# Two stages of a Flamingo block: the last store of keys and values crosses the stage border, one weight split moves two tiles forward, one signal moves ahead of four loads

## The reference, cut to what matters

```python
x = x + tanh(g_xattn[0]) * L0_xattn(_layernorm(x), ctx, ...)     # stages 1, 2, 3
x = x + tanh(g_ffn[0])   * L0_ffn(_layernorm(x), ...)            # stages 4, 5
x = x + tanh(g_xattn[1]) * L1_xattn(_layernorm(x), ctx, ctx)     # stage 6
x = x + tanh(g_ffn[1])   * L1_ffn(_layernorm(x), ...)            # stage 7

# L0_xattn, 16 query heads over 4 key and value heads, head size 128:
q = rope(rms_norm(x @ wq)); k = rope(rms_norm(x @ wk)); v = x @ wv
k_ctx = rms_norm(ctx @ wk_ctx); v_ctx = ctx @ wv_ctx
p = softmax(q @ [k_ctx, k].T / sqrt(128) + causal)
out = (p @ [v_ctx, v]) @ wo
```

## Time and profile before

| | |
|---|---|
| median of three runs | 2157.63 us |
| the three runs | 2154.73, 2157.63, 2162.49 us |
| the profiled execution | 2155.77 us |
| its span in the profile | 2154.0 us |
| TensorE busy | 1963.9 us, 91% of the span |
| mean granted clock of TensorE | 0.967 of full speed |

### The profile page before, as it was taken

How to read it: one execution, slowest core, us unless ns; L and a number is a source line. 1 busy time by engine, 2 the same in 40 slices (tenths; PEclk the granted TensorE clock), 3 DMA queues, 4 the chain that set the end, 5 groups by cost and what they waited for, 6 DMA issues and landing times. The chain is left out here.

```text
span 2154.0 us, 33149 instructions
## 1 busy us (share of the span) xinstructions
PE 1963.9 (91%) x10498; PEld 1491.0 (69%) x10514; DVE 1344.3 (62%) x2408; ACT 1072.4 (50%) x2590; POOL 428.9 (20%) x515
## 2 busy tenths in 40 slices
PE   6999789999999999978998999999979978886898
PEld 5788667777777777756887778778768865554444
DVE  6777566666666666654342755555645437884886
ACT  3333356666656666653222312222324328984998
POOL 1111144444444444430000000000000001222111
PEclk9999899999999999999999999999989988997999
DMA  6776843333323240118443121112477422331121
GB/s 252 260 256 221 293 129 108 79 89 79 96 74 108 60 107 22 30 30 293 136 142 112 59 79 39 59 39 88 127 255 258 157 85 89 108 108 46 35 59 44
DMA packets 209016, 253.55 MB, mean 118 GB/s; under 512 B 12246, under 2 KB 158822, under 8 KB 202476
## 3 DMA queue, kind: packets, MB, share of 16 engines
q1 hardware_dynamic: 208876, 251.82, 36.7%
HBM read 151.10 MB, written 100.68 MB: 117 GB/s over the span
## 5 line engine op out<-in xcount | busy, mean ns | idle before, releaser
L966 ACT ACTIVATE at_prob<-at_S,at_bias,at_rq 128x384 f32<-128x384 f32 (+1 forms) x256 | 184.1, 731 | 142.9 <-DVE at_bias L1051 138.1
L1062 DVE TENSOR_TENSOR at_pt_lo<-at_PT,at_pt_hi 128x512 fp32r<-128x512 f32 x224 | 148.8, 688 | 92.3 <-ACT at_pt_hi L973 92.2
L835 POOL TENSOR_SCALAR at_prob<-at_prob,at_rsum 128x384 f32<-128x384 f32 (+1 forms) x256 | 160.3, 639 | 135.0 <-DVE at_rsum L1057 135.0
L1713 ACT ACTIVATE gu_silu<-gu_G 128x512 f32<-128x512 f32 x64 | 38.1, 596 | 245.3 <-PE gu_G L103 236.0
L1042 DVE TENSOR_REDUCE at_nmax<-at_S 128x1 f32<-128x384 f32 (+1 forms) x256 | 150.9, 617 | 9.5 <-PE at_S L885 5.5
L973 ACT ACTIVATE at_pt_hi<-at_PT 128x512 fp32r<-128x512 f32 x224 | 127.9, 604 | 53.8 <-PE at_PT L892 53.8
L892 PE MATMUL at_PT<-c_ident,at_prob 128*128 128x128 f32 x896 | 127.8, 277 | 21.1 <-DVE at_pt_lo L1062 20.8
L1750 DVE TENSOR_TENSOR gu_h<-gu_silu,gu_U 128x512 f32<-128x512 f32 x64 | 43.8, 686 | 151.6 <-PE gu_U L103 105.2
L824 POOL TENSOR_TENSOR at_q<-at_by_cos,at_by_sin 128x512 f32<-128x512 f32 x64 | 82.1, 1283 | 265.0 <-DVE at_by_sin L1034 152.5
L892 PEld LDWEIGHTS at_PT<-c_ident,at_prob 128*128 128x128 f32 x896 | 97.8, 140 | 50.9 <-DVE at_pt_lo L1062 46.5
L881 PE MATMUL at_S<-at_k_hi,at_q_hi 128*128 128x384 f32 (+1 forms) x256 | 113.2, 442 | 15.5 <-DVE at_q_lo L1067 11.5
(11 more groups left out here) (341 smaller groups left out, 5474.7 us busy)
## 6 DMA issues: line engine op xcount, KB each, us to landing
wide<-at_ot SPq DMA_DIRECT2D x64, 256.0 KB, 2.9
wide<-gu_h SPq DMA_DIRECT2D x64, 256.0 KB, 3.2
o_a<-wide SPq DMA_DIRECT2D x14, 1024.0 KB, 4.8
d_a<-wide SPq DMA_DIRECT2D x13, 1024.0 KB, 8.6
keys_hi<-kv_kt_hi SPq DMA_DIRECT2D x16, 512.0 KB, 3.3
keys_lo<-kv_kt_lo SPq DMA_DIRECT2D x16, 512.0 KB, 4.1
values_hi<-kv_v_hi SPq DMA_DIRECT2D x16, 512.0 KB, 4.7
values_lo<-kv_v_lo SPq DMA_DIRECT2D x16, 512.0 KB, 5.0
```

What stands on the lines that cost most here:

```text
L835: pool.tensor_scalar(prob[u % 2][:, h, 0:n], prob[u % 2][:, h, 0:n], rsum[:, s:s + 1], 1.0, ALU.mult, ALU.mult).then_inc(normed.sem, 1)
L966: act.activation(prob[u % 2][:, h, 0:n], S[h][:, 0:n], ACT.Exp, bias=bias[:, s:s + 1], scale=rq[u % 4][:, h:h + 1], accum_out=sums[:, s:s ...
L1062: dve.tensor_tensor(pt_lo[f % 4][:], bank_of("p", u, kb)[:], pt_hi[f % 4][:].bitcast(F32), ALU.subtract).then_inc(pt_done.sem, 1)
```

## The change

Four things change; the arithmetic and all values stay as they are.

- **Stores.** The last four stores of stage 1 (turn 3, n = 8) signal a semaphore of their own, `c.kv_last`, which stage 1 doesn't wait for. The buffers that they read (`kt_hi`, `kt_lo`, `v_hi`, `v_lo` of source 0) move to the right side and live through stage 2. There they serve as `prob`, `pt_hi` and `pt_lo`. SP waits for `kv_last` in stage 2, ahead of the loads of `wq` into `prob`.
- **Split.** The high and low parts of the first `wq` piece are taken after tile 5 of the last turn, not after tile 7.
- **Signal.** `xt_arrived` is signalled ahead of the four small loads.
- **keep_awake** at the end of stage 1 has 12 matmuls, not 24.

```diff
@@ keys_values
-        kt_hi = [mem.sb(f"kt_hi{s}", [P, HKV, TOK]) for s in range(SRC)]
-        kt_lo = [mem.sb(f"kt_lo{s}", [P, HKV, TOK]) for s in range(SRC)]
+        kt_hi = [c.kt_hi, mem.sb("kt_hi1", [P, HKV, TOK])]
+        kt_lo = [c.kt_lo, mem.sb("kt_lo1", [P, HKV, TOK])]
...
+        v_hi = [c.v_hi, mem.sb("v_hi1", [P, TT, HKV * HD], F32R)]
+        v_lo = [c.v_lo, mem.sb("v_lo1", [P, TT, HKV * HD], F32R)]
...
+                    stored = kv_stored[s].sem if more or n < NT else c.kv_last
                     wait_apart(sp, kt_done, turn, n, passed)
                     for dram, keys in ((scr.k_hi, kt_hi), (scr.k_lo, kt_lo)):
-                        sp.dma_start(dram[turn, s, :, :, tok], keys[s][:, :, tok]).then_inc(kv_stored[s].sem, 16)
+                        sp.dma_start(dram[turn, s, :, :, tok], keys[s][:, :, tok]).then_inc(stored, 16)
...
-            for s in (xt_stored, ct_stored, *kv_stored):
+            for s in (xt_stored, ct_stored, kv_stored[1]):
                 sp.wait_ge(s.sem, s.per * (PAIRS + 1))
+            sp.wait_ge(*kv_stored[0].at(PAIRS - 1, 64))
...
-            keep_awake(pe, T[0], c, 2 * AWAKE)
+            keep_awake(pe, T[0], c, AWAKE)
...
+            def split_queries_hi(i):
+                act.wait_ge(wq_arrived[i], 16)
+                act.wait_ge(*V_full.at(PAIRS - 1, TT))
+                act.activation(c.wq_hi[i][:], (x, cx)[i][:], ACT.Copy).then_inc(wq_hi_done, 1)
...
+                    if not more and i == TT + 1:
+                        split_queries_hi(0)
...
-            for i in range(2):
-                act.wait_ge(wq_arrived[i], 16)
-                act.wait_ge(*V_full.at(PAIRS - 1, TT))
-                act.activation(c.wq_hi[i][:], (x, cx)[i][:], ACT.Copy).then_inc(wq_hi_done, 1)
+            split_queries_hi(1)
...
+            def split_queries_lo(i):
+                dve.wait_ge(wq_hi_done, i + 1)
+                dve.tensor_tensor(c.wq_lo[i][:], (x, cx)[i][:], c.wq_hi[i][:].bitcast(F32),
+                                  ALU.subtract).then_inc(wq_lo_done, 1)
...
+                    if not more and i == TT + 1:
+                        split_queries_lo(0)
...
+            split_queries_lo(1)
@@ attention
+        mem.sems.append(c.kv_last)
...
-        prob = [mem.sb(f"prob{i}", [P, GROUP, 2 * L]) for i in range(2)]
+        prob = [c.kt_hi, c.kt_lo]
...
-        pt_hi = [mem.sb(f"pt_hi{i}", [P, GROUP * P], F32R) for i in range(4)]
-        pt_lo = [mem.sb(f"pt_lo{i}", [P, GROUP * P], F32R) for i in range(4)]
+        pt_hi = [c.v_hi[:, i, :] for i in range(4)]
+        pt_lo = [c.v_lo[:, i, :] for i in range(4)]
...
+            for b in range(2):
+                sp.sem_inc(xt_arrived[b].sem, 32)
             sp.dma_start(cosw[:], io["c_cos_tok"]).then_inc(setup, 16)
...
-            for b in range(2):
-                sp.sem_inc(xt_arrived[b].sem, 32)
             load_kv(0, 0, 0)
+
+            sp.wait_ge(c.kv_last, 4 * 16)
             for n in range(HKV - AHEAD):
                 weights.load(sp, n)
@@ make_queries
+        self.kt_hi, self.kt_lo = (far(f"kt_{part}", [P, HKV, TOK], F32) for part in ("hi", "lo"))
+        self.v_hi, self.v_lo = (far(f"v_{part}", [P, TT, HKV * HD]) for part in ("hi", "lo"))
+        self.kv_last = nc.alloc_semaphore("queries_kv_last")
```

More of the change, by code:

```diff
@@ L289, in keys_values @@
         kn = [mem.sb(f"kn{i}", [P, 512]) for i in range(2)]
-        v_hi = [mem.sb(f"v_hi{s}", [P, TT, HKV * HD], F32R) for s in range(SRC)]
-        v_lo = [mem.sb(f"v_lo{s}", [P, TT, HKV * HD], F32R) for s in range(SRC)]
+        v_hi = [c.v_hi, mem.sb("v_hi1", [P, TT, HKV * HD], F32R)]
+        v_lo = [c.v_lo, mem.sb("v_lo1", [P, TT, HKV * HD], F32R)]
         cosw = mem.sb("cosw", [P, 2, HD])
@@ L396, in body @@
                         sp.dma_start(dram[turn, s, :, tiles, :],
-                                     values[s][:, tiles, :].bitcast(F32)).then_inc(kv_stored[s].sem, 16)
+                                     values[s][:, tiles, :].bitcast(F32)).then_inc(stored, 16)
                     if more and n == TT:
@@ L912, in values @@
                 s, own = 1 if kb < 2 else 0, (slice(None), 2 * b + kb % 2, slice(g * HD, (g + 1) * HD))
-                three_passes(pe, O[:], [(v_hi[s][own], v_lo[s][own], pt_hi[f % 4][:], pt_lo[f % 4][:])],
+                three_passes(pe, O[:], [(v_hi[s][own], v_lo[s][own], pt_hi[f % 4], pt_lo[f % 4])],
                              start=(kb == 0), stop=(kb == blocks[u] - 1)).then_inc(PV_done.sem, 1)
@@ L972, in keep_probs @@
                 act.wait_ge(*PV_done.at(turn, f - 3))
-                act.activation(pt_hi[f % 4][:], bank_of("p", u, kb)[:], ACT.Copy).then_inc(pt_hi_done.sem, 1)
+                act.activation(pt_hi[f % 4], bank_of("p", u, kb)[:], ACT.Copy).then_inc(pt_hi_done.sem, 1)
             def keep_queries(turn, u):
@@ L1061, in split_probs @@
                 dve.wait_ge(*pt_hi_done.at(turn, f + 1))
-                dve.tensor_tensor(pt_lo[f % 4][:], bank_of("p", u, kb)[:], pt_hi[f % 4][:].bitcast(F32),
+                dve.tensor_tensor(pt_lo[f % 4], bank_of("p", u, kb)[:], pt_hi[f % 4].bitcast(F32),
                                   ALU.subtract).then_inc(pt_done.sem, 1)
@@ L2617, in make_queries, with far @@
         self.queries = ExitStack()
-        def far(name, shape):
-            return self.queries.enter_context(nc.sbuf_tensor("queries_" + name, shape, F32R, side="right"))
+        def far(name, shape, dt=F32R):
+            return self.queries.enter_context(nc.sbuf_tensor("queries_" + name, shape, dt, side="right"))
         self.wq_hi = [far(f"wq_hi{i}", [P, DC, 512]) for i in range(2)]
         self.wq_lo = [far(f"wq_lo{i}", [P, DC, 512]) for i in range(2)]
+        self.kt_hi, self.kt_lo = (far(f"kt_{part}", [P, HKV, TOK], F32) for part in ("hi", "lo"))
+        self.v_hi, self.v_lo = (far(f"v_{part}", [P, TT, HKV * HD]) for part in ("hi", "lo"))
+        self.kv_last = nc.alloc_semaphore("queries_kv_last")
         self.xt_hi = far("xt_hi", [P, DC, TOK])
```

## The result

| | before | changed |
|---|---|---|
| median | 2154.40 us (20 runs) | 2147.30 us (20 runs) |
| spread | 2147.14 to 2164.03 | 2143.00 to 2153.07 |
| ratio, 95% interval | | 0.9966 [0.9954, 0.9978] |
| profiled execution, its span | 2155.77, 2154.0 | 2143.13, 2141.4 |

The changed kernel is 0.34% faster, 7.3 us by the ratio, with 4.7 to 9.9 us in the interval. The sum of the prediction was 5.7 us, 0.26%. Measured again later, beside two other versions, the same kernel came to 0.9983 [0.9969, 0.9996] (12 runs). The mean of the two ratios is 0.9974, 5.5 us. The two profiled executions, though, lie 12.6 us apart. So there is the border to read, and then a difference twice as large as the one between the medians.

A forecast was written before the change was run, and what follows sets the result against it. Stage 2 was taken as a steady loop behind TensorE, so a border saving is kept whole. 3.85 + 1.85 = 5.7 us off 2155.77 gives 2150.1, off the runs' median 2151.9; forecast 2151, range 2147 to 2157 us.

The forecast's parts named there:

- The border, 3.85 us: Between stages 1 and 2: without the wait for the last store, stage 2's first load is issued 3.85 us sooner.
- The delay of 1.3 us on tile 6: VectorE, stage 1: the early split makes tile 6 1.3 us late; idle time before tile 7 takes all but 0.1.
- The signal, 1.85 us: Start of stage 2: signalled ahead of four small loads, TensorE's first product and the rotation come 1.85 us sooner.
- rival A: Start of stage 2: small loads queue, the mask lands late, the rotation waits for its tables; gain 3.85 to 4.9, chance 0.2.
- The new wait costs nothing: SP in stage 2: it reaches `kv_last` at 250.6, the stores land at about 245.4, 5 us of cover.
- Rival D: SP in stage 2: stores landing late hold it at `kv_last`, outweighing the gain after 257; 2159 us for 260, chance 0.03.
- The clock, zero: TensorE's first product after the border: still 1.2 GHz expected, effect -0.7 to +1.6 us, taken as zero.
- the prediction's own signs: Stage 2: rotation 8.1 us, not 13.8, after SP's last store ends; high parts start at 258.9, not 264.6.
- The 2.8 and 4.7 us: TensorE in stage 2: two slow-clock stretches after idle time, taken to agree with a release point varying from run to run.
- "By it the halved `keep_awake` buys nothing", and 12 off the path: End of stage 1: 12 matmuls end at 239.0, before SP; 24 would end 0.3 us after; no gain for stage 2.
- The pieces' landing as a cap: Stage 2: the two other `wq` pieces' loads just fit; shortening TensorE's part further is worth at most 0.7 us more.
- Rival C: Border: the barrier waits for transfers in flight, so only 1.85 us is left; 2154 us, chance 0.08.

The follow-up runs named there:

- Versions 2 and 4: 2: the changed kernel with both first weight pieces split after the last tile again, 2149.68 us; 4: it with the last store awaited before the border, 2152.29 us.
- version 1: The changed kernel with the tokens' signal behind the four small loads again; 2148.76 us.
- versions 6 and 7: 6: version 3 with stage 2's two weight pieces loaded first, 2147.64 us; 7: that plus 14 readerless matmuls after the first product, 2147.18 us.
- version 3: The changed kernel with 24 instead of 12 small matmuls at the end of stage 1; 2143.02 us, timed later at ratio 0.9980.
- the wide fill: The version with both fills, its 38 fill matmuls now 512 columns wide, with half the added instructions; 2145.31 us, ratio 0.9950 to the kernel before.
- the version with both fills: 24 matmuls, weight pieces first, plus 14 and 24 readerless matmuls in TensorE's two idle stretches; 2147.60 us, timed later at ratio 0.9985 to the kernel before.

## Why the prediction was right

The forecast was 5.7 us and 2151 us, with most of the chance on a difference within 0.3%. The range, 2147 to 2157 us, held the time of 2147.30, but only by 0.3 us. The forecast of 2151 was 3.7 us too high. Of this 2.3 us are the base: the forecast started from three runs of the kernel before, and over 20 runs its median is 2154.40; from there the sum gives 2148.7. The measured ratio lies just past 0.3%, a side to which the prediction gave 0.31 and not its 0.64. Its interval and the second measurement's share 0.22% to 0.31%, where the 0.26% of the sum lies. So the mechanism of the border and of the signal is borne out; the clock's share was misjudged, and that the time fell inside the range is in part luck. By steps:

- **The border, 3.85 us: right.** 3.71 us. SP is last, VectorE ends just below it, 12 matmuls are off the path. Versions 2 and 4 price the parts: 1.6 us for the split, 3.8 for the store.
- **The delay of 1.3 us on tile 6, absorbed before the last stores: right**; it was 1.2, and the last store moved by 0.03.
- **The signal, 1.85 us: right.** 1.72 us in the profile, 2.0 by version 1. The mask didn't hold the rotation. The prediction saw next to no slack, and there were 1.8 us: 0.9 from the slow product, and 0.7 since the mask landed 2.7 us after its issue, not 3.4 as before. With a fast product (versions 6 and 7) the rotation does wait for the tables, which is rival A's wait.
- **The new wait costs nothing: right**, with 4.5 us of cover. Rival D never had ground: the last store landed 5.4 us after its issue, and D needed 17.
- **The clock, zero: the size was off, and in both directions.** Both products were slow throughout, 1.4 us of loss at ScalarE's high parts (4.06 us gained there, not 5.7), and behind them the second unit's scores gave 1.1 back. At the third unit 5.2 us are left of 3.71 + 1.72 = 5.4, so the term sums to -0.2. That it is so near zero is luck: two terms over 1 us cancel, and I had not counted the third slow stretch at all. By the prediction's own signs the rotation came 9.3 us after the last store's issue ended, not 8.1, and the high parts at 260.55, not 258.9. The 2.8 and 4.7 us that were read as a point of release that varies were two stretches of one execution; between executions the runs show it better, with six slow matmuls at the start of the first product in the kernel before, ten in the changed one and all twelve in version 1.
- **"By it the halved `keep_awake` buys nothing", and 12 off the path: half right.** It buys nothing, and it may also cost: 24 fit at the border without the 0.3 us that I charged for them (version 3), and after the shorter idle time the product began at full clock in six of seven profiles. In the measured time the two numbers of matmuls can't be told apart (0.9980 and 0.9983).
- **The pieces' landing as a cap: right**, shown by version 3's wait.
- **Rival C falls** (SP issues at 243.90 with the stores in flight until 245.6).
- **What I left out** is scatter of single executions: stage 6 by 6 us (8 with the kernel before), the crossing by 1.3 us for the same kernel (24 matmuls), stage 1 by 2.4. It is the reason why 5.5 us need 20 runs.

## What to carry to other kernels

A store at a stage's end needn't be waited for if its buffer lives on; wait where the room is written again. But look who is next: here another engine would have ended 2.0 us later, and 1.6 of the 3.7 us would have stayed there. When a chain gets shorter, read the landings of what it meets next: two loads that had waited unseen were the limit once TensorE was faster. Count from a common event near the change: 5 us can't be read from the ends of two profiles that scatter by 6 us and more in a stage nobody touched. And before a longer stretch is put down to more instructions, look at the clock granted in it.

## What the runs showed of the hardware that I had not expected

- After 2.4 us of idle time the first product began at full clock in six of seven profiles, and in two of these it fell to 1.2 GHz after four or five matmuls, in the midst of dense work; in the seventh, that of the wide fill, it began slow. After 5.1 us or more it began at 1.2 GHz in all seven.
- At the one jump back in its list TensorE stood still for 1.7 to 2.7 us in all 14 profiles, with no releaser named. What differed more was what came behind: full clock in six, 1.2 GHz for about 3 us in six and for about 7 us in two, with the two units taking 23.5 to 23.7, 23.9 to 24.9, and 26.6 and 26.8 us. The two are those of the version with both fills. Whether its longer code has a part in that is open: version 7, with 28 of those 76 more matmul records ahead of the loop, kept the full clock.
- The last of the first eight loads (128 KB each) took 7.7 to 8.4 us to land when it stood behind the two weight pieces (1 MB each), and 3.3 to 5.8 us in the nine profiles where it stood ahead of them. That held TensorE up for 1.7 to 3.4 us, in all five profiles with the pieces first.
